# VectorE takes half of the score evacuation from ScalarE in a float32 cross-attention kernel

## The reference, cut to what matters

```python
# x: (16, 128, 512) queries; ctx: (16, 2048, 512) keys and values; 16 heads of 32
qh = (layernorm(x) @ wq + bq)  ->  heads          # 128 queries per batch
kh = (ctx @ wk + bk)           ->  heads          # 2048 keys per batch
vh = (ctx @ wv + bv)           ->  heads
attn = einsum('bhqd,bhkd->bhqk', qh, kh) / sqrt(32)
out = einsum('bhqk,bhkd->bhqd', softmax(attn, axis=-1), vh)
x = x + out @ wo + bo
```

## Time and profile before

| | |
|---|---|
| median of 3 runs | 3285.53 us |
| lowest, highest | 3280.8, 3290.76 us |
| the profiled execution, its own time | 3291.81 us |
| its span, first to last instruction | 3290.0 us |
| mean granted clock of TensorE | 0.986 |
| PE busy | 3192.8 us (97%) |
| PEld busy | 2619.5 us (80%) |
| DVE busy | 2343.9 us (71%) |
| ACT busy | 1729.1 us (53%) |
| POOL busy | 2132.2 us (65%) |

### The profile page before, as it was taken

The page is one execution under the profiler, slowest core; times in us unless marked ns, Lnnn a source line. Parts: engine busy times, 40 slices in busy tenths (PEclk is TensorE's granted clock), DMA queues, the critical chain, the costliest instruction groups (busy, mean ns, idle before and its releaser), DMA issues.

```text
span 3290.0 us, 76145 instructions
## 1 busy us (share of the span) xinstructions
PE 3192.8 (97%) x29818; PEld 2619.5 (80%) x29818; DVE 2343.9 (71%) x3307; ACT 1729.1 (53%) x2338; POOL 2132.2 (65%) x1520
## 2 busy tenths in 40 slices
PE   8999999999999999999999999948999999999999
PEld 7788888888888888888888888736888888888888
DVE  6466666666666666666666666666887688799997
ACT  3566666766766766666666666632123322321111
POOL 3388888888888888888888888754555000033332
PEclk9999999999999999999999999968999999999999
DMA  5111211222212212212122122122223432310000
GB/s 164 49 54 52 62 60 52 64 60 59 64 54 58 61 52 62 60 52 63 58 56 64 52 67 61 47 68 98 74 94 105 136 103 91 126 55 24 22 19 20
DMA packets 232372, 217.44 MB, mean 66 GB/s; under 512 B 17392, under 2 KB 181104, under 8 KB 230896
## 3 DMA queue, kind: packets, MB, share of 16 engines
q1 hardware_dynamic: 232048, 212.88, 21.0%
HBM read 174.41 MB, written 38.40 MB: 65 GB/s over the span
## 4 chain that ended last, share of the span: by engine, by line
PE 88%; DVE 4%; ACT 3%; issue 3%; DMA 1%; POOL 1%; SPq 0%; ACTq 0%; POOLq 0%; DVEq 0%
PE a_bank L103 70%; PE a_bank L1655 9%; PE a_bank L1671 4%; ACT x_s L1390 2%; PE a_bank L1693 2%; PE a_bank L1682 1%; PE a_bank L866 1%; PE a_bank L1700 1%; PE a_bank L2614 1%; PE a_bank L877 1%; PE a_bank L941 0%; DMA x_staged<-shifts 0%; PE a_bank L915 0%; POOL x_pairs L1285 0%; PE a_bank L2587 0%
## 5 line engine op out<-in xcount | busy, mean ns | idle before, releaser
L103 PE MATMUL a_bank<-x_ctx,x_wk 128*128 128x512 f32 x3072 | 812.0, 405 | 0.0
L103 PE MATMUL a_bank<-x_wv,x_ctx 128*128 128x512 f32 x3072 | 742.0, 391 | 0.0
L103 PEld LDWEIGHTS a_bank<-x_wv,x_ctx 128*128 128x128 f32 x3072 | 578.0, 188 | 124.6
L103 PEld LDWEIGHTS a_bank<-x_ctx,x_wk 128*128 128x128 f32 x3072 | 551.1, 189 | 119.7 <-issue 0.2
L1529 DVE TENSOR_TENSOR x_s<-x_s,a_bank 128x1024 f32<-128x1024 f32 x512 | 610.2, 1213 | 25.4 <-ACT a_bank L1397 25.4
L1285 POOL TENSOR_TENSOR x_pairs<-x_pairs,x_s 128x1024 f32<-128x1024 f32 x256 | 613.0, 2394 | 20.1
L1390 ACT ACTIVATE x_s<-a_bank 128x1024 f32<-128x1024 f32 x512 | 497.0, 1022 | 184.9 <-PE a_bank L1655 184.9
L1403 ACT ACTIVATE x_s<-x_s 128x1024 f32<-128x1024 f32 x512 | 527.6, 1055 | 97.8 <-DVE x_s L1529 97.4
L1282 POOL TENSOR_TENSOR x_pairs<-x_s 128x1024 f32<-128x1024 f32 x128 | 303.2, 2369 | 250.0 <-ACT x_s L1403 250.0
L1502 DVE TENSOR_TENSOR a_bank<-a_bank,x_s 128x1024 f32<-128x1024 f32 x256 | 302.6, 1228 | 86.3 <-ACT x_s L1390 86.3
L1655 PEld LDWEIGHTS a_bank<-x_q,x_k 32*128 32x128 f32 x8192 | 253.8, 187 | 105.7 <-issue 64.1
(11 more groups left out here) (201 smaller groups left out, 4629.8 us busy)
## 6 DMA issues: line engine op xcount, KB each, us to landing
x_tile_raw<-in_ctx SPq DMA_DIRECT2D x248, 256.0 KB, 3.8
x_staged<-shifts SPq DMA_DIRECT2D x128, 256.0 KB, 3.4
m_ff_src<-in_w_ff SPq DMA_DIRECT2D x44, 192.0 KB, 2.5
wq_ff<-m_ff_dst SPq DMA_DIRECT2D x44, 192.0 KB, 1.8
s_attT<-attT SPq DMA_DIRECT2D x16, 512.0 KB, 4.3
m_w_raw<-in_w SPq DMA_DIRECT2D x32, 256.0 KB, 3.0
f_w_in<-wq_ff SPq DMA_DIRECT2D x22, 256.0 KB, 3.2
q_x<-in_x SPq DMA_DIRECT2D x16, 256.0 KB, 4.2
```

Of the source, the lines that this page charges most:

```text
L103: mm = pe.matmul(out, lhs[a], rhs[b], start=first and n == 0, stop=last and n == 2)
```

## The change

Heads 2 and 3 of both halves go from ScalarE to DVE. ScalarE's `keep_scores` makes one copy per half; DVE gets a `keep_scores` of its own that makes the other and raises `folded`. `kept` now counts 2 per block and `folded` 5: copy of half 0, copy of half 1, fold of heads 0 and 1, fold of heads 2 and 3, reduction. In DVE's step the copy of half 0 stands first, and the copy of half 1 between `add_shift(e1, 0)` and `fold(s, 0)`. PE's half 1 waits for one count of each semaphore; its half 0 waits for `kept` alone. The arithmetic, the transfers and the buffers are the same.

```diff
-    FOLDS = 3
+    FOLDS = 5
+    KEPT = 2
...
             def keep_scores(s, h):
                 act.wait_ge(scored, START + s.count(2, h + 1))
...
-                for two in (slice(0, 2), slice(2, HG)):
-                    act.activation(scores_of(s)[:, two, cols(h, TPC)],
-                                   bank[:, two].rearrange("p j (t s) -> p j t s", t=TPC), ACT.Copy).then_inc(kept, 1)
+                act.activation(scores_of(s)[:, 0:2, cols(h, TPC)],
+                               bank[:, 0:2].rearrange("p j (t s) -> p j t s", t=TPC), ACT.Copy).then_inc(kept, 1)
...
+            def keep_scores(s, h):
+
+                dve.wait_ge(scored, START + s.count(2, h + 1))
+                used = s.back(RING)
+                if h == 0 and used.exists():
+                    dve.wait_ge(pv_done, START + used.count(1, 1))
+                    dve.wait_ge(summed, START + used.count(SUMS, SUMS - 1))
+                dve.tensor_copy(scores_of(s)[:, 2:HG, cols(h, TPC)],
+                                bank[:, 2:HG].rearrange("p j (t s) -> p j t s", t=TPC)).then_inc(folded, 1)
+
             def fold(s, h):
 
-                dve.wait_ge(kept, START + s.count(HG, 3 + h))
+                if h:
+                    dve.wait_ge(folded, START + s.count(FOLDS, 2))
+                else:
+                    dve.wait_ge(kept, START + s.count(KEPT, 2))
...
-                dve.wait_ge(folded, START + s.count(FOLDS, 2))
+                dve.wait_ge(folded, START + s.count(FOLDS, 4))
...
                 dens = e3.exists() and e3.group % 2
+                if s.exists():
+                    keep_scores(s, 0)
                 if e2.exists():
                     gather(s, e2)
...
                 if s.exists():
+                    keep_scores(s, 1)
                     fold(s, 0)
                     fold(s, 1)
                     fold_tiles(s)
...
                 if h:
-                    pe.wait_ge(kept, START + s.count(HG, 2))
+                    pe.wait_ge(kept, START + s.count(KEPT, 1))
+                    pe.wait_ge(folded, START + s.count(FOLDS, 1))
                 elif s.back(1).exists():
-                    pe.wait_ge(kept, START + s.count(HG))
+                    pe.wait_ge(kept, START + s.count(KEPT))
```

More of the change, by code:

```diff
@@ L1792, in _ @@
             late.turn_input(pe, FIRST)
-            pe.wait_ge(kept, START + HG * BLOCKS)
+            pe.wait_ge(kept, START + KEPT * BLOCKS)
             late.queries(pe, FIRST)
```

## The result

The changed kernel takes 3323.73 us (median of 4 runs, 3320.54 to 3327.04); before it was 3288.15 us beside these runs (3280.8 to 3292.47). The ratio is 1.0111 with a 95% interval of 1.0088 to 1.0133: slower by 36 us. The forecast was 33 us slower (3318 us, range 3299 to 3345).

What follows compares the result with a forecast made beforehand. PE, with 88% of the chain of waits, was taken as the bound, so only when it is held counts. Block changes averaging 0.27 us over 125 blocks gave 33 us on 3285.5, hence 3318 us, range 3299 to 3345.

Steps and rivals of the forecast that it cites:

- The copy of half 1 inside the closed chain: VectorE's unbroken work from first addition to PE's turn: folds +0.64 us with `sum_up`, +0.15 or +0.07 without.
- The copy of half 0 in VectorE's idle time: First in VectorE's step, before the gathering: costs nothing; PE's half 1 starts 0.36 us earlier in blocks without `sum_up`.
- The price of the copy: VectorE's new copy of 1024 elements from PSUM: taken as a `tensor_tensor` of that shape, 1.21 us, 1.13 start to start.
- equal 415 ns: VectorE's copy and `tensor_tensor` of 256 elements take the same time, taken as a sign of float32's single rate from PSUM.
- rival A: VectorE's copy runs at two elements a cycle, about 0.48 us less: -0.15 us a block, 3267 us; chance 0.05.
- PE's margin: Slack at PE's turns of folds and column before a later VectorE delays it; called thin, +0.64 us becoming +0.45 or +0.64.
- rival B: PE's margin at the two turns is deeper, so +0.64 us is absorbed: -10 to +9 us, around 3287; chance 0.11.
- the block of 2051: Block in the earlier trace with folds 1.11 us late, PE's turn 0.87 late; 0.93 stayed, a sign that delays pass on.
- Rival C: Larger delay from missing overlap, PSUM slowdown or late exponentials: 0.1 to 0.25 us a block; 3343 us at +0.2; chance 0.19.
- The sum: Four equally frequent block kinds, +0.45, +0.64, -0.06, +0.04: 0.27 us a block times 125 blocks, 33 us.

Runs made afterwards that it cites:

- e1: Kernel before, with only the copy of heads 2 and 3 of half 0 moved to VectorE, both copies of half 1 staying with ScalarE: 3266.89 us, ratio 0.9926.
- e2: Kernel before, with only the copy of heads 2 and 3 of half 1 moved to VectorE, both copies of half 0 staying with ScalarE: 3344.38 us, ratio 1.0168.
- e4: Changed kernel, with VectorE copying half 1 twice, the second behind the first's semaphore: 3478.74 us, ratio 1.0572 to the kernel before.
- e6: Changed kernel, reordered: VectorE copies half 1 and folds before adding to head 0; ScalarE's first exponential follows its second value item: 3280.26 us, ratio 0.9975 to before.
- e5: Changed kernel plus 64 semaphore increments nobody waits for, ahead of VectorE's first block: 3318.08 us, ratio 1.0093 to the kernel before.
- e7: Kernel with only half 0's copy on VectorE, plus 64 idle semaphore increments ahead of VectorE's first block: 3273.65 us, ratio 0.9954 to before.

## Why the prediction was right

*The copy of half 1 inside the closed chain* was the step that carried the sum, and it holds: +0.64 us in the folds was forecast, 0.65 measured; e1 without it is fast, e2 with it and without the copy of half 0 is slower than the whole change, e4 adds a second one in full, and e6, with the same copy but one addition fewer in front of PE's turn, gains.

*The copy of half 0 in VectorE's idle time* was costed at nothing, and its gain, 0.36 us for PE's half 1, at 0.06 of it once VectorE held PE at the turn. Both right in kind: half 1 starts 0.25 us earlier (2.98, not 2.87, us), and e1 shows 0.28 us to be had in each block without `sum_up` when the chain is not made longer. Why PE needs 0.11 us more than the start of `sum_up` suggested is open; no wait for another engine stands in front of it, and in the changed kernel it has no price, since PE is held later anyway.

*The price of the copy*, 1.21 us by the equal 415 ns of copy and `tensor_tensor`, is measured at 1.222 us; rival A falls. The Trainium skill, "VectorE: DVE Perf Modes", section "Why PSUM operands drop a tier", agrees: float32 from PSUM goes at the single rate. The prediction's estimate of 1.19 us was 0.03 short. Rival A's saving was mis-summed: with the slope of 1.04 ns it is 0.53 us, not 0.48, and its +0.13 becomes +0.11; its price stays near -0.15 us a block.

*PE's margin* (rival B) is 0.2 us in blocks with `sum_up` of the first half of keys, as the block of 2051 had let expect; that its late fold was a stall of VectorE does not change what it shows of PE. In the second half the margin is 0.04 us: PE follows VectorE by 0.05 us where it is held, and not by the 0.09 of the earlier trace rows, so the forecast of +0.64 us came out as +0.61 and +0.62. *Rival C*, a second limit, did not come: even in e4 each block grows by just the copy and its semaphore, 1.25 to 1.27 us.

*The sum*: from the third block's start to that of the 126th the changed kernel needs 2026.71 us, the kernel before 1994.67, which is 32.0 over 123 blocks; forecast were 33 over 125. What the sum left out are single events that nearly cancel in the profiled executions: the first block starts 6.1 us earlier, the first two blocks are 4.4 us shorter, and after the 126th block's start 9.4 us are added: -6.1 - 4.4 + 32.0 + 9.4 = 30.9, the difference of the spans.

Most of these events do not belong to the change. In the set-up of the kernel before, PE waits 3.98 us for VectorE at 41.4 us and has a granted clock of 0.50 from 40.5 to 47 us, where the changed kernel has neither; over all kernels here the first block starts between 97.0 and 103.1 us, and the copies are not yet at work there. About 3 of the 4.4 us are the lower clock in the second block shown under e1. Of the 9.4 us, 6.8 are the block of the 5.9 us stall, which e5 does not have. So the agreement of 33 and 36 to 3 us is partly luck; that of the 0.27 us a block is not.

## What to carry to other kernels

Before work is moved to an engine that is less busy, draw the chain of that engine between two meetings with the bounding engine, and ask whether the moved instruction falls into an idle stretch of it or into the chain. Here one of two equal copies fell into 2 us of idle time (worth -25 us alone, 17 of them in the repeated blocks) and its twin into a chain with 0.4 to 0.6 us of room (+53 us alone); moving only the first, e1_first_half, beats both kernels at 0.9926 of the time before. Where both must be moved, another order of the same work can take something else out of the chain for the copy that went in (0.9975).

## What the runs showed of the hardware that was not expected

VectorE stands still once in the block phase of most of these kernels with no semaphore to wait for: 5.9 us in the changed kernel and none of 0.5 us or more in e5, 2.4 us in e1 and 10.0 in e7. In each of these pairs only 64 increments ahead of the first block differ. In this kernel a difference of 4 to 7 us (0.2%) between two profiled executions came from the place of such a stall alone; compare the stretches without it.

Behind a wait of PE of 2.23 us, TensorE's granted clock was at its lower level for some 6 us in the kernel before, which made that block about 3 us longer. So a difference in the first blocks is compared only after the granted clock of both.

VectorE and ScalarE copy out of different PSUM banks at the same time at their usual speeds: both from 1145.70 us in e1, VectorE in 1.23 and ScalarE in 1.02 us, the time that its copy takes alone.
